# Graph network kernel: the convolutions' loops over eight groups of edges a turn instead of four

## What is computed

```python
def conv(h, W, b):
    m = jnp.concatenate([h[dst], h[src], edge_attr], axis=1) @ W + b
    return jax.ops.segment_sum(m, dst, num_segments=n_nodes)
h = jax.nn.relu(conv(x, W1, b1))
h = jax.nn.relu(conv(h, W2, b2))
return conv(h, W3, b3)
```

## Time and profile before

| | us |
|---|---|
| median of 3 runs | 8589.94 (8589.36 to 8590.86) |
| span of the profiled execution | 12711.1 |
| TensorE products busy | 8189.4 |
| TensorE weight loads busy | 6348.8 |
| VectorE busy | 4579.9 |
| ScalarE busy | 2257.6 |
| GpSimd busy | 5682.2 |

### The profile page before, as it was taken

The page is one execution under the profiler, slowest core; times in us unless marked ns, Lnnn a source line. Parts: engine busy times, 40 slices in busy tenths (PEclk is TensorE's granted clock), DMA queues, the critical chain, the costliest instruction groups (busy, mean ns, idle before and its releaser), DMA issues. The chain is left out here.

```text
span 12711.1 us, 171279 instructions
## 1 busy us (share of the span) xinstructions
PE 8189.4 (64%) x53894; PEld 6348.8 (50%) x53895; DVE 4579.9 (36%) x6263; ACT 2257.6 (18%) x3537; POOL 5682.2 (45%) x5876
## 2 busy tenths in 40 slices
PE   4777777677776777755656665566556556656565
PEld 3555555566565666544444444444344444444443
DVE  5555555211112111123333333333433333333334
ACT  3444444000000000011111111111211111111112
POOL 3444444444444444444445444444244444444442
PEclk8888888777777777767777777777777777777777
DMA  4333434555555555541111111111111111111111
GB/s 137 147 139 139 150 139 139 193 180 177 180 179 178 179 177 174 178 138 43 39 43 45 43 41 45 42 40 43 55 41 43 42 42 45 42 41 42 42 43 50
DMA packets 417816, 1230.97 MB, mean 97 GB/s; under 512 B 122166, under 2 KB 221853, under 8 KB 369103
## 3 DMA queue, kind: packets, MB, share of 16 engines
q1 hardware_dynamic: 217352, 748.98, 16.7%
q0 software_dynamic: 187232, 233.06, 7.9%
q10 hardware_dynamic: 13160, 248.05, 4.9%
HBM read 948.11 MB, written 281.51 MB: 97 GB/s over the span
## 5 line engine op out<-in xcount | busy, mean ns | idle before, releaser
L1856 POOL DMA_INDIRECT data<-q_rows,idx x3328 | 3149.7, 946 | 3771.1 <-ACT idx L1983 2641.5
L904 POOL DMA_INDIRECT data<-h_parts,idx x2508 | 2494.5, 995 | 3040.7 <-PE p_part L919 1168.7
L1028 PE MATMUL p_z<-hs,adj 128*128 128x192 bf16 x22442 | 2674.8, 276 | 827.9 <-issue 819.8
L1028 PEld LDWEIGHTS p_z<-hs,adj 128*128 128x128 bf16 x22442 | 2197.2, 110 | 1394.0 <-issue 1187.5
L2058 DVE TENSOR_TENSOR_SCAN run<-reset,run,p_turn 128x1024 f32<-128x1024 bf16 x416 | 976.4, 2347 | 2771.2 <-DMA h<-h_rows 2293.9
L1876 PE MATMUL p_back<-ident,run 128*128 128x128 f32 x3344 | 608.6, 342 | 1355.7 <-DVE run L2058 1328.8
L1876 PEld LDWEIGHTS p_back<-ident,run 128*128 128x128 f32 x3344 | 511.0, 180 | 1742.7 <-issue 1742.3
L1988 ACT COPY back<-p_back 128x1024 f32<-128x1024 f32 x418 | 423.0, 1012 | 5188.0 <-PE p_back L1876 3377.7
L1887 PE MATMUL part<-hot,back 128*128 128x128 f32 x6688 | 998.0, 302 | 500.5 <-issue 290.2
L1882 PE MATMUL part<-hot,t 128*128 128x128 f32 x6688 | 1061.4, 326 | 282.7 <-issue 282.7
L1882 PEld LDWEIGHTS part<-hot,t 128*128 128x128 f32 x6688 | 1032.0, 243 | 297.3 <-issue 297.3
(11 more groups left out here) (308 smaller groups left out, 6421.1 us busy)
## 6 DMA issues: line engine op xcount, KB each, us to landing
adj<-counted SPq DMA_DIRECT2D x304, 1568.0 KB
counted<-adj ACTq DMA_DIRECT2D x76, 3136.0 KB
reset<-flags SPq DMA_DIRECT2D x208, 512.0 KB
data<-q_rows,idx POOLq DMA_INDIRECT x3328
data<-h_parts,idx POOLq DMA_INDIRECT x2508
feat<-in_ea_blocks SPq DMA_DIRECT2D x208, 128.0 KB
ea<-in_ea_cols SPq DMA_DIRECT2D x154, 88.0 KB
rden<-node_rows SPq DMA_DIRECT2D x50, 256.0 KB
```

Source lines behind the costliest of these rows:

```text
L904: pool.indirect_dma_start(out=data[:, p, j, 0:PARTS], out_offset=None, in_=table[:, :], in_offset=bass.IndirectOffsetOnAxis(ap=idx[:, p, j ...
L1028: mm = pe.matmul(p_z[:, 0:PARTS], adj[:, (q + LAG) % 2, hi, :], hs[:, hi, :], start=(hi == 0), stop=(hi == BLOCKS - 1))
L1856: pool.indirect_dma_start(out=data[:, r, j, :], out_offset=None, in_=q_rows[:, :], in_offset=bass.IndirectOffsetOnAxis(ap=idx[:, r, j:j + ...
```

## The change

A turn has eight groups, four E and four P in alternation, and there are 19 turns. `data` has as many slots as P positions in layers 1 and 2 (four); in layer 0 it keeps two (`HELD`), shared by positions 1 and 5, and 3 and 7, and GpSimd's wait on `s_part` counts accordingly. The index tiles and the semaphores `s_idx` and `s_row` follow the P positions, so there are four of each. In layers 1 and 2 the block of counts for the E group two ahead is loaded by the general rule q + 2, into slot q % 2. The number of groups, their size and the order P and E stay.

```diff
--- before.py
+++ after.py
@@ -44,14 +44,14 @@
 KC = D + 3 * FE + 1
 
 GC = 11
-KINDS = "EPEP"
+KINDS = "EPEPEPEP"
 TURN = len(KINDS)
 POS_P = [p for p in range(TURN) if KINDS[p] == "P"]
 POS_E = [p for p in range(TURN) if KINDS[p] == "E"]
 OF_E = slice(POS_E[0], None, 2)
 OF_P = slice(POS_P[0], None, 2)
 NQ = len(POS_E)
-KT = 38
+KT = 19
 NGC = TURN * KT
 NE = NQ * KT
 GEC = GC * P
@@ -695,7 +695,8 @@
     with ExitStack() as ctx:
         sb, ps, sem = chip.scope(ctx)
         idx = sb("idx", [P, len(POS_P), GC], I32)
-        data = sb("data", [P, len(POS_P), GC, WIDE], BF16)
+        HELD = 2 if first else len(POS_P)
+        data = sb("data", [P, HELD, GC, WIDE], BF16)
         rare_idx = sb("rare_idx", [P, GC], I32)
         rare_data = sb("rare_data", [P, GC, WIDE], BF16)
         rare_hot = sb("rare_hot", [P, GC, P], BF16)
@@ -835,10 +836,10 @@
                     else:
                         sp.wait_ge(s_mid, k * NQ + (q + 1))
                     gate(sp)
-                    if not isinstance(k, int):
-                        bring(q, bass.ds(k * NQ + (NQ + q), 1), half)
-                    elif q == 0 and not last:
-                        bring(q, slice(0, 1), half)
+                    if not isinstance(k, int) or q + 2 < NQ:
+                        bring(q % 2, bass.ds(k * NQ + (q + 2), 1), half)
+                    elif q + 2 == NQ and not last:
+                        bring(0, slice(0, 1), half)
 
             def further(k, pos, m, x):
                 sp.wait_ge(s_added_x, x)
@@ -881,7 +882,7 @@
             finished_quads(sp, quads_of(sp, chip.quads, KT - 1), store)
             if not last:
                 for half in (0, 1):
-                    sp.wait_ge(s_load[0][half], 16 if first else 16 * KT + 16)
+                    sp.wait_ge(s_load[0][half], 16 if first else 16 * (NE // 2) + 16)
             sp.wait_ge(s_out, 32 + 16 * QUADS)
         @block.gpsimd
         def _(pool):
@@ -898,11 +899,11 @@
             with pool.Fori(0, KT) as k:
                 for p, pos in enumerate(POS_P):
                     pool.wait_ge(s_idx[p], k + 1)
-                    pool.wait_ge(s_part, k * H + (nth[pos] + 1))
+                    pool.wait_ge(s_part, k * H + (H + nth[pos] + 1 - HELD * (H // len(POS_P))))
                     gate(pool)
                     for j in range(GC):
                         pool.indirect_dma_start(
-                            out=data[:, p, j, 0:PARTS], out_offset=None, in_=table[:, :],
+                            out=data[:, p % HELD, j, 0:PARTS], out_offset=None, in_=table[:, :],
                             in_offset=bass.IndirectOffsetOnAxis(ap=idx[:, p, j:j + 1], axis=0),
                         ).then_inc(s_row[p], 16)
 
@@ -911,7 +912,7 @@
             columns = lambda pos: slice(0, WIDE) if pos in POS_P else slice(PARTS, PARTS + EA)
 
             def rows_of_edges(pos, slot, j):
-                return data[:, slot, j, :] if slot is not None else dense_ea[:, j, 0:EA]
+                return data[:, slot % HELD, j, :] if slot is not None else dense_ea[:, j, 0:EA]
 
             def products(pos, slot):
                 par = nth[pos] % 2
@@ -1225,7 +1226,7 @@
 
             def split_ea(k, n):
                 b, pos = n % 2, hots[n % H]
-                to = data[:, POS_P.index(pos), :, PARTS:] if pos in POS_P else dense_ea
+                to = data[:, POS_P.index(pos) % HELD, :, PARTS:] if pos in POS_P else dense_ea
                 v.wait_ge(s_ea[b], k * (16 * TURN // 2) + 16 * (n // 2 + 1))
                 split_in_three(ea[:, b], to, s_ea_step, k * (4 * TURN) + 4 * n)
```

## The result

The changed kernel takes 8502.2 us (8493.7 to 8507.2) where the kernel before, on the same chip, takes 8589.65 (8581.9 to 8590.9): ratio 0.9901, interval 0.9889 to 0.9912. That is 87 us less; 111 were forecast. The profiled execution of after spans 8505.5 us. The profile of before spans 12711.1 us.

What follows compares the result with a forecast made beforehand. The chain TensorE, VectorE, ScalarE was taken to bound the first convolution, GpSimd the other two. Ends 63 and clock 43 make 106 us, plus 5 us, slots nothing: 8589.94 - 111 = 8479 us, range 8377 to 8576.

Steps and rivals of the forecast that it cites:

- 4121 us of the profile are not there when nothing is recorded: Whole kernel: profile span of 12711.1 us against 8589.94 us plain, the difference of 4121 us laid to recording.
- Gap of an end, 3.33 us: First convolution, end of a turn: TensorE saves 3.33 us per removed end, 63 us for 19.
- Clock, 2.25 us for each end: First convolution, behind a turn's end: TensorE at half clock for 4.5 us loses 2.25 us, 43 us for 19 ends.
- A body, once fetched, is kept: All three loops: code isn't fetched anew each turn, since the trace has fewer code packets (35 and 37) than 114 turns.
- Rival 4: Loops' jumps: doubled body fetched anew every turn, at least 1.7 us per exposed fetch, 8576 to 8867 us; chance 0.09.
- packets "well above 72": Whole kernel: code packets rising well above 72 would show the prediction wrong.
- GpSimd leads in the second and third convolution: There GpSimd's 27.6 us a turn exceed TensorE's 26.4, so removed ends save only 5 us for both passes.
- Rival 1: Second and third convolution: TensorE leads there too, 64 us come on top of 106, 8420 us; chance 0.20.
- GpSimd gets at most 5 us ahead, and two slots hold that: Second and third convolution: TensorE's longest interval, 18 to 19 us, against 13.8 of gathers, so four data slots bring nothing.
- the finished nodes of the last turn: End of each convolution: two blocks of nodes stay behind the loop before and after the change, costing nothing.
- the bound of 30 each: Second and third convolution: shortening by more than 30 us each would show the prediction wrong.
- Rival 2: First convolution: only the gap is saved, not the clock, or VectorE takes half of it; 8522 us, chance 0.17.

Runs made afterwards that it cites:

- e0_before: The kernel before, unchanged, profiled again on a chip of the faster kind; 8583.3 us span recorded, 8583.9 us unrecorded.
- e10: The changed kernel with 50 one-element memsets ahead of VectorE's loop in the first convolution, on a faster chip; 8457.4 us, ratio 0.9856 to the kernel before.
- e4: The changed kernel once more, nothing added, on a chip of the slower kind; 12920.6 us, ratio 1.0138 to the kernel before.
- e6: The changed kernel with 10 one-element memsets ahead of VectorE's loop in the first convolution, on a slower chip; 12910.6 us, ratio 1.014 to the kernel before.
- e2_later_only: The kernel before with turns of eight and four slots in the second and third convolution alone; 8545.7 us, ratio 0.9958.
- e3: The changed kernel with two data slots in all three convolutions; 8550.2 us, ratio 0.9968 to the kernel before.

## Why the prediction was right or wrong

**"4121 us of the profile are not there when nothing is recorded": wrong.** e0_before spans 8583.3 us while recorded, and before takes 8583.9 unrecorded on that chip; on the slower kind it takes 12698 us and more unrecorded. So recording costs nothing that can be seen, and the difference was the chip. The choice of undisturbed turns that was built on it still gave the gap of an end, alike on both kinds (6.92 and 6.94 us). It did not give the clock, nor the whole intervals (22.6 us over an inside position in that trace, 18.4 in e0_before). And the forecast that the recorded span falls by more than the plain time failed (8583.3 - 8505.5 = 78 against 87), and no case allowed that the sign could turn from chip to chip, as it did.

**Gap of an end, 3.33 us: right.** 6.94 us from window to next count in e0_before against the 6.92 taken, and in after 55 of 57 inside positions at 18.41 to 18.76 us.

**Clock, 2.25 us for each end: too high.** 4.6 us for the whole end leave 1.3. The stretch taken had the lower level throughout; in e0_before's it came for part of it (0.53 to 0.68 behind all 14 ends without nodes). It wasn't typical even of its own trace, where 10 of 14 such stretches have 0.71 or more. The measured value lay between the bounds of 0 and 4.5. Term: 87 us, not 106.

**"A body, once fetched, is kept": half wrong, the largest miss.** TensorE's body stays, 44 packets of 16 KB. VectorE's doesn't: 47.6 us in the first convolution, shown by e10 in time and by the packets of e4 to e6. Rival 4 had named VectorE and "at least 1.7 us" for an exposed fetch; it is 2.6. It put 57 turns behind it, and there were 18 with a price, since in the second and third convolution the body stays (e2_later_only has 44 packets of q14). The prediction's own sign of failure, packets "well above 72", stands in after's page: 184. A body of 354 instructions was fetched anew, in packets of 8 KB, when it touched four of them, and stayed when it touched three. The Trainium skill ("Runtime: NRT & Kernel Launch", Instruction fetch mechanics) has the mechanism, a jump out of what is kept waits for a fetch, and the trace agrees with it (2.6 to 2.9 us). It gives 32 KiB, 512 instructions, for engines other than TensorE, in blocks of 16 KiB. Four packets of 8 KB are 32 KB, three for the body and one fetched ahead, so the size may well hold; the blocks were half as large here, and a body below 512 instructions was not for that alone kept.

**GpSimd leads in the second and third convolution: right.** Rival 1, TensorE leading, is excluded: 1.25 us for each gather where nothing stops it, and fewer ends alone (e3) bring nothing there. Forecast for them were 5 us; measured are 13 us lost in the two passes (4 and 9). The term that the prediction put at nothing is the finished nodes of the last turn, four blocks behind the last gather instead of two, some 10 us a pass.

**"GpSimd gets at most 5 us ahead, and two slots hold that": wrong.** The sum compared one long interval of TensorE with one group of gathers. But e0_before has a wait of 10.2 us at the start of the pass and more after blocks of nodes, and a leader that is stopped doesn't make it good: the gathers take 36 us longer than in after, as much as its gaps over 1.4 us. These gaps, 37 us in the second pass and 26 in the third, bounded the gain; e3 puts it at 31 and 24. That TensorE's lag adds up over several turns is how I explain them; it was not followed turn by turn. The term was some 50 us, not 0. The stages shorten by 27 and 15 us, so the bound of 30 each that was to show a failure was not passed: it was set too wide to catch this.

**Sum.** 87 for the ends - 48 for VectorE's code + 42 in the later passes (55 for the slots - 13 for fewer ends alone) = 81 us; the spans give 78 (8583.3 - 8505.5) and the medians 87, against 106 + 0 + 5 = 111. The range held the time because two misses of opposite sign and like size stood in it, not because the account was right. Rival 2's 8522 us and the price of the fetch in the range are what covered it.

## What to carry to other kernels

Before a profile's span is compared with a time, make sure that both come from the same kind of chip: here the recorder was blamed for a difference of half the time that it had no part in. When a loop body grows, count the code packets of each engine and look at the first step behind the jump, not of TensorE alone: a body can be short enough by its length and still touch one packet too many, and shifting it is worth trying. Where one engine leads a pass, any wait of that engine is lost for good: cost more buffers by the leader's summed waits in a clean trace, not by one interval. And when turns grow, count what the last turn leaves to do after the leader has finished; nothing hides it.

## What the runs showed of the hardware

- One kernel takes 8582 to 8590 us in three comparisons and 12698, 12731 and 13149 in three others, on other chips, and one change has ratios 0.9901 and 1.0138 on a chip of each kind.
- VectorE behaves as if three packets of 128 instructions were kept for a loop, with one more fetched ahead: five packets a turn for a body over four, none for the same body over three. The number of places is read from the counts of e4 to e6 and e10, not measured by itself, and 128 is the estimate above.
- A jump whose code has to come costs VectorE 2.6 to 2.9 us (17 of 18 jumps in after), and cost this kernel 2.6 us of its time each (after against e10).
- GpSimd's indirect gathers of 128 rows follow each other at 1.25 us, of which 0.944 is the gather, on both kinds of chip. TensorE's body of more than 1356 instructions (the count in the prediction) stayed.
